# Gated delta-rule attention with a routed feed-forward: 128 blocks written out with constant waits, and the queries' rows moved by POOL's queue

## What is computed

```python
q = short_conv(x @ Wq)                      # 8 heads of 128, 4-tap causal convolution, then silu
k = short_conv(x @ Wk)                      # 3 keys for each token and head
v = short_conv(x @ Wv)                      # 3 values for each token and head
q, k = l2norm(q) * d ** -0.5, l2norm(k)
for each token t:                           # state S: 128x128 for each batch and head
    S = S * exp(g[t])
    for i in range(3):
        S = S + beta[t, i] * outer(k[t, i], v[t, i] - k[t, i] @ S)
    o[t] = q[t] @ S
o = rmsnorm(o) * rms_weight * silu(x @ Wg)
x = layernorm(x + o @ Wo)
x = layernorm(x + experts(x))               # 8 experts of width 816, the best 2 for each token
```

## Time and profile before

| what | us |
|---|---|
| median of 3 runs | 4982.57 |
| lowest and highest run | 4980.44, 4993.09 |
| span of the profiled execution | 4978.8 |
| PE, DVE, ACT, POOL busy in it | 4230.5, 3658.3, 3285.0, 1648.1 |
| first and last `gate` of the 128 blocks | 133.9, 3943.2 |

### The profile page before, as it was taken

One profiled execution on the slowest core, in us unless ns is written; L12 is line 12 of the kernel. 1 busy time (PEld: TensorE's weight loads), 2 busy tenths in 40 slices (PEclk: granted clock), 3 DMA queues, 4 the chain that ended last, 5 costly groups with the idle time before them and its releaser, 6 DMA issues. The chain is left out here.

```text
span 4978.8 us, 148669 instructions
## 1 busy us (share of the span) xinstructions
PE 4230.5 (85%) x47876; PEld 3759.0 (75%) x47876; DVE 3658.3 (73%) x10194; ACT 3285.0 (66%) x9028; POOL 1648.1 (33%) x1615
## 2 busy tenths in 40 slices
PE   2889988989898888898888898889889867599992
PEld 1788878888887777788788787888878745488882
DVE  6888888888888778788888788888888722344446
ACT  3777777777777677777777777777777611255552
POOL 3434333334433333343334343333434202200004
PEclk6999999999999999999999999999999877699996
DMA  6232223222223333222222222322222133366664
GB/s 234 69 95 73 66 77 86 79 70 77 77 71 70 76 77 70 70 77 79 82 75 77 77 67 77 92 76 67 75 77 75 43 88 108 123 236 227 230 236 140
DMA packets 363269, 490.64 MB, mean 99 GB/s; under 512 B 94080, under 2 KB 308096, under 8 KB 343680
## 3 DMA queue, kind: packets, MB, share of 16 engines
q1 hardware_dynamic: 304784, 437.06, 29.8%
q10 hardware_dynamic: 51568, 27.04, 1.9%
q0 software_dynamic: 6144, 16.79, 1.1%
HBM read 352.02 MB, written 107.75 MB: 92 GB/s over the span
## 5 line engine op out<-in xcount | busy, mean ns | idle before, releaser
L1134 DVE SCALAR_TENSOR_TENSOR conv_acc<-bank,c_cur,conv_acc 128x256 f32<-128x256 f32 x2688 | 1265.9, 477 | 274.3 <-ACT conv_acc L944 261.2
L692 PE MATMUL bank<-x_cur,w_cur 128*128 128x259 f16 (+1 forms) x6144 | 913.2, 288 | 29.4 <-DVE v_rows L1122 26.3
L1329 POOL TENSOR_TENSOR squares<-kq_t 128x768 f32<-128x768 f32 x128 | 187.7, 1467 | 1909.4 <-ACT kq_t L955 1909.4
L1195 DVE CAST_PREDICATED xs_lev<-mask,bank 128x256 f16<-128x256 uint16 x1536 | 662.2, 431 | 198.1 <-PE bank L756 174.4
L1002 ACT ACTIVATE invt<-bank 128x256 f16<-128x256 f32 x1280 | 509.7, 398 | 400.3 <-issue 374.5
L993 ACT ACTIVATE inv<-bank 128x256 f16<-128x256 f32 x1536 | 607.0, 395 | 167.8 <-PE bank L768 158.1
L692 PEld LDWEIGHTS bank<-x_cur,w_cur 128*128 128x128 f16 (+1 forms) x6144 | 577.7, 102 | 124.7 <-DVE v_rows L1122 27.2
L780 PE MATMUL bank<-invt,xs_lev 128*128 128x64 f16 x5120 | 379.9, 199 | 309.4 <-ACT invt L1002 305.2
L780 PEld LDWEIGHTS bank<-invt,xs_lev 128*128 128x128 f16 x5120 | 293.2, 101 | 341.5 <-ACT invt L1002 254.2
L944 ACT ACTIVATE conv_acc<-bank,c_cur 128x256 f32<-128x256 f32 x896 | 425.3, 475 | 156.5 <-PE bank L692 149.4
L824 PE MATMUL bank<-w_sol,k_rows 128*128 128x128 f32 x2048 | 474.6, 315 | 4.5 <-ACT w_sol L1012 4.1
(11 more groups left out here) (241 smaller groups left out, 10672.6 us busy)
## 6 DMA issues: line engine op xcount, KB each, us to landing
w_cur<-w_parts_scratch SPq DMA_DIRECT2D x128, 1024.0 KB, 7.1
ew<-e_parts_scratch SPq DMA_DIRECT2D x117, 896.0 KB, 6.2
x_cur<-x_parts_scratch SPq DMA_DIRECT2D x128, 259.0 KB, 7.0
x_slots<-no_rows SPq DMA_DIRECT2D x128, 256.0 KB, 7.1
e_parts_scratch<-e_pair SPq DMA_DIRECT2D x96, 224.0 KB, 6.0
o_rows<-w_sol ACTq DMA_DIRECT2D x512, 32.0 KB, 4.6
y_scratch<-y_buf SPq DMA_DIRECT2D x128, 128.0 KB, 6.3
y_in<-y_scratch SPq DMA_DIRECT2D x32, 512.0 KB, 4.1
```

The costliest lines, as they stand in the source:

```text
L692: last = mm(bank[i % 2][:, 0:PW], w_cur[k.i % 2][:, wp, kt, c * P:(c + 1) * P].bitcast(BF16 if wp else F16), x_cur[k.i % 2][:, xp, kt, 0:P ...
L1134: v.scalar_tensor_tensor(acc, bank[at % 2][:, i:i + TB], c_cur[k.i % 2][:, c, i:i + 1], acc, ALU.mult, ALU.add).then_inc(tap_step.sem if i ...
L1195: v.copy_predicated(half(xs_lev[g][l - 1][:], l, 0), half(mask4[:, l], l, 0).bitcast(U16), packed(halves(LEVX), l)).then_inc(x_kept.sem, 1)
```

## The change

The change does three things. Every engine's 128 blocks are written out, so all counts and addresses are constants, and the registers and loops are gone. The three copies for each block (`c_cur`, `g_cur`, `t_cur`) go, and their readers read `conv_sb`, `g_parts` and `tables` themselves; SP's additional waits and counts go with them. And `move_outputs` moves from ACT's order to POOL's, between `g_rows` and `square`, with the same transfers and the same waits.

```diff
 class Block:
-    def __init__(self, i, m, s, size):
-        self.i, self.m, self.size = i - s, m, size
-        self.n = i - s if m is None else size * m + (i - s)
-        self.runs = m is not None or 0 <= i - s < NIT
+    def __init__(self, n):
+        self.n = self.i = n
+        self.runs = 0 <= n < NIT
+        self.h, self.place = n % H, n % (B * H) * NTB + n // (B * H)
...
-            def run_bodies(eng, body):
-                assert NIT % UNROLL == 0 and UNROLL >= STAGES
-                for i in range(UNROLL):
-                    body(*blocks(i, None, UNROLL))
-                with eng.Fori(1, NIT // UNROLL) as m:
-                    for i in range(UNROLL):
-                        body(*blocks(i, m, UNROLL))
-                for i in range(NIT, NIT + STAGES - 1):
-                    body(*blocks(i, None, UNROLL))
+            def run_bodies(body):
+                for i in range(NIT + STAGES - 1):
+                    body(*blocks(i))
...
                         sp.dma_start(w_cur[res][:].rearrange("p a b c -> p (a b c)"), w_dram[h]).then_inc(loaded[res], 16)
-                        sp.dma_start(c_cur[res][:], conv_sb[:, h]).then_inc(loaded[res], 16)
-                        sp.dma_start(g_cur[res][:], g_parts[:].rearrange("p n a -> p (n a)")[:, bass.ds((head * NTB + tb) * UN, UN)])\
-                            .then_inc(loaded[res], 16)
...
-                    def body(tb, head, new=True):
-                        n = B * H * tb + head
-                        if new:
-                            done(sp, stated, 7, n - 8)
-                            sp.sem_inc(sp_waited, 1)
-                            sp.dma_start(t_cur[head % 8][:].rearrange("p a b -> p (a b)"),
...
                     def load_next(tb, head):
                         n = B * H * tb + head
                         done(sp, projected, 7, n - 1)
-                        sp.sem_inc(sp_waited, 1)
                         done(sp, tapped, 6, n - 1)
-                        sp.sem_inc(sp_waited, 1)
-                        at_least(sp, g_made, n)
-                        sp.sem_inc(sp_waited, 1)
...
-                    @at_stage
-                    def move_outputs(k):
-                        done(act, sol_kept, 7, k.n)
-                        at_least(act, scaled, k.n - 1)
-                        act.sem_inc(act_waited, 1)
-                        for c in range(4):
-                            act.dma_start(o_rows[k.i % 2][c * CH:(c + 1) * CH], w_sol[k.i % 2][96:128, c::4, :]).then_inc(moved[k.i % 2], 16)
...
                         keep_t(4, 0, k1)
-                        move_outputs(k3)
                         keep_tt(4, 0, k1)
...
+                    @at_stage
+                    def move_outputs(k):
+                        done(pool, sol_kept, 7, k.n)
+                        at_least(pool, scaled, k.n - 1)
+                        for c in range(4):
+                            nc.gpsimd.dma_start(o_rows[k.i % 2][c * CH:(c + 1) * CH], w_sol[k.i % 2][96:128, c::4, :]).then_inc(moved[k.i % 2], 16)
...
                         square_q(k1)
                         g_rows(k0)
+                        move_outputs(k3)
                         square(k0)
```

More of the change, by code:

```diff
@@ L67 @@
 STORED = 5
-UNROLL = 32
 WR = 3
@@ L461, in done @@
             def done(eng, count, key, n, *more):
-                if not isinstance(n, int) or n >= 0:
+                if n >= 0:
                     eng.wait_ge(count.sem, count.upto(max((key,) + more, key=lambda k: count.upto(k, NIT // 2)), n))
@@ L530, in build, with blocks @@
             class Block:
[L533 to L536 removed]
+                def __init__(self, n):
+                    self.n = self.i = n
+                    self.runs = 0 <= n < NIT
+                    self.h, self.place = n % H, n % (B * H) * NTB + n // (B * H)
                 def turn(self, ring):
[L540 to L543 removed]
+                    return self.n // ring
+            def blocks(i):
+                return [Block(i - s) for s in range(STAGES)]
             def at_stage(f):
@@ L649, in _ @@
                     load(0, 0, 0)
[L650 to L657, removed]
-                            load_next(tb, head)
[L659 to L667, removed]
+                    for n in range(NIT):
+                        tb, head = n // (B * H), n % (B * H)
+                        if n + 1 < NIT:
+                            load_next(tb, head)
+                        outputs(tb, head)
+                        pieces(tb, head)
+                    for i in range(STORED):
                         outputs(NTB, i, new=False)
@@ L929, in _ @@
                     pe.wait_ge(zeroed, 1)
-                    run_bodies(pe, body)
+                    run_bodies(body)
                 @block.scalar
@@ L1105, in _ @@
                     act.wait_ge(zeroed, 1)
-                    run_bodies(act, body)
+                    run_bodies(body)
                 @block.vector
@@ L1300, in body @@
                         mask_x(2, 0, k0)
-                    run_bodies(dve, body)
+                    run_bodies(body)
                 @block.gpsimd
@@ L1309, in g_rows @@
                     def g_rows(k):
-                        pool.wait_ge(loaded[k.i % 2], 64 * (k.turn(2) + 1))
                         done(pool, tt_made, "decays", k.n - 1)
-                        tt(g_upto[:], g_cur[k.i % 2][0:96, :, None].broadcast_to([96, UN, CH]),
+                        tt(g_upto[:], g_parts[0:96, k.place, :, None].broadcast_to([96, UN, CH]),
                            uptob[0:96, None, 0:CH].broadcast_to([96, UN, CH]), ALU.mult).then_inc(g_made, 1)
@@ L1381, in body @@
                         scale_outputs(k3)
-                    for head in range(B * H):
-                        body(0, head, *blocks(head, None, B * H))
-                    with pool.Fori(1, NTB) as tb:
-                        for head in range(B * H):
-                            body(tb, head, *blocks(head, tb, B * H))
-                    for i in range(NIT, NIT + STAGES - 1):
-                        body(None, i, *blocks(i, None, B * H))
+                    for i in range(NIT + STAGES - 1):
+                        body(*((i // (B * H), i % (B * H)) if i < NIT else (None, i)), *blocks(i))
         attention_scope.close()
```

52 lines of the change are left out of this document (18 added, 34 removed).

## The result

| | before | after |
|---|---|---|
| median of 4 runs, us | 4981.5 | 5201.1 |
| lowest and highest | 4950.0, 4993.1 | 5184.7, 5216.3 |
| span of the profiled execution | 4978.8 | 5214.5 |
| last `gate` of the 128 blocks | 3943.2 | 4173.3 |

The changed kernel is slower: the ratio is 1.045, with an interval of 1.041 to 1.049. I had forecast 4685 us, faster. The loss lies in the blocks. (Further down, the kernel "squares later" has its time from its three runs within 1.5% of its fastest; its profile is of the fourth, slower one, 4967 us.) `gate` now runs from 133.9 to 4173.3 us, so the blocks take 4039.4 us, 230 more than the earlier trace rows give.

What follows compares the result with a forecast made beforehand. The prediction took ACT's issuing of the moves, with PE's slow clock, and the transfers' landing as the bound. Block gain 252 plus written-out blocks 43 made 295 us off 4978.8, so 4684 span, forecast 4685 us, range 4540 to 4850.

Steps and rivals of the forecast that it cites:

- What bounds the kernel: In the blocks, the 8.1 us from first move issue to squaring: ACT's work, delayed by issuing and slow clock, and the transfers.
- ACT without the moves: Without issuing, ACT's copy starts 3.30 us earlier and ACT reaches the squaring 4.5 us after the first issue, not 8.1.
- POOL issues the moves: POOL's four issues before its squares, at most 1.26 us each, fit its 14.51 us of idle time at no cost.
- My estimate of 5430: By the skill page's 3.1 us a POOL step, rows would land at 12 us, giving some 5430 us; no separate chance.
- When the rows land: POOL steps of 1.1 us put the fourth issue at 3.3 us; with 2.8 us of landing, rows land at 6.1 us.
- the transfers land as late as ACT's: Rival, chance 0.17: landing stays 4.6 us, rows come at 7.9 us, a block gains 0.2 us, time 4915 us.
- The gain of a block: First issue to squaring shrinks from 8.1 to 6.1 us: 2.0 us a block, 252 us in 126 blocks.
- slower: Rival, chance 0.08: POOL's issues become the serial part; 2.0 us steps and 3.5 us landing give 5116 us.
- The clock: After PE's shorter stall of about 1.2 us, in place of 2.4, the clock was assumed to stay at its upper level.
- back to 4875: Failure case: the clock still falls after the shorter stall, costing up to 1.5 us a block, 190 us in all.
- Written-out blocks: Removing the loops' two jumps saves 13 us, and half of 60 us in the other loop steps 30: 43 us together.
- Fewer transfers on SP: Three of SP's nine issues a block go, of 2 to 16 KB; worth nothing, since SP is ahead of the others.

Runs made afterwards that it cites:

- squares later: Changed kernel, but ACT squares the moved rows seven instructions later, with PE's norms and DVE's sum later too: 4912.1 us, 0.982 of the kernel before.
- the kernel with held loads: Changed kernel, but SP issues the next block's input and weight loads only after a block's four moves have landed: 4445.3 us, 0.890 of the kernel before.
- the experiments with matmuls in the stall: Changed kernel with channel 4's projection, just ahead of PE's stall, computed four times or twice (18 or 6 matmuls more): 4959.8 and 5079.4 us.
- the kernel without moves: Changed kernel without the four moves, the rows' buffers set to one, so the outputs are wrong: 4520.2 us, 0.903 of the kernel before.

## Why the prediction was wrong, by its steps

*What bounds the kernel.* Right: the stretch from the first issue to the squaring, and that under ACT's stall the landing lies at nearly the same time. Incomplete: I took DVE for the next bound, 26.4 us a block. The floor is PE's: 3201 us busy in 127 blocks is 25.2, and the kernel with held loads has a median step of 25.2. It is so low because PE's busy time itself shrinks at full clock, 3400 to 3201.

*ACT without the moves.* Right: the copy came early, the old waits of 374.5 and 305.2 us are gone, and ACT arrives 4.0 us after the first issue (median), where I took 4.5. Ten instructions of ACT stand between the moves' old place and the squaring, not eleven.

*POOL issues the moves.* Mis-sized in the good direction: a step of 0.54 us, not 1.1. The indirect transfer was a poor neighbour for a direct one. The squares weren't late (9.4 us after the first issue in the block shown, 10.1 before in that of the earlier trace rows). The Trainium skill's SBUF — State Buffer page ("A bandwidth-pool intuition that's wrong") has a transfer by POOL that takes about 620 ns alone take about 3100 ns beside a VectorE copy. My estimate of 5430 took that as the step between issues. Nothing of the kind shows here: no issue of the 512 took over 0.774 us, and with the load held the landing has a median of 1.8 us, though VectorE is busy for 3123 of 3262 us.

*When the rows land.* This step failed first. I put "2.8 us" from issue to landing, with 0.4 us for the load; it was 4.7 in the median and 5.9 for the fourth. What sets it is SP's load (with what SP issues behind it), not who issues: with the load held, POOL's lands in 1.8 us and ACT's in 1.9. The rows I leaned on the earlier trace rows compared POOL's transfers with SP's in another stretch and of another size. The Trainium skill (DMA: Bandwidth & Descriptors, "Issuing engines are not separate DMA queues") says that transfers of all engines run on the same 16 DMA engines; the trace agrees, with 4.7 against 4.6 us. In the prediction this was the rival "the transfers land as late as ACT's", to which I gave 0.17.

*The gain of a block.* By my own sum the measured landing leaves 8.1 - 7.5 = 0.6 us a block, some 76 us, and that rival, with 0.2 us, said 4915. The kernel is 286 us slower than even this. So the landing alone explains no loss. The chance of "slower", 0.08, was for another mechanism, long issues by POOL, and that one didn't happen.

*The clock.* This step failed second, and it decided the sign: "I assume that so short a stall leaves the clock at its upper level". The stall wasn't short. ACT arrives 3.3 us earlier than before (4.0 in place of 7.3 us after the first issue) and the rows 0.5, so ACT's wait for them grows from 0.9 to 3.4 us a block, and PE stands 357 / 110 = 3.2 us in place of 2.4. And the dips of the clock are longer (8.4 us against 4.0 on average) and more. I had priced the case "back to 4875", with the clock no worse than before; the experiments with matmuls in the stall show that the dearer clock is worth at least the 241 us that they give back. PE's additional busy time, 187 us, is part of that.

*Written-out blocks.* 43 us predicted, 26 measured. The jumps' 13 us are in it; of the other 60 us, of which I had taken half, some 13 came back.

*Fewer transfers on SP.* At nothing, in the sum, and nothing speaks against it. The profile seems to say that `w_cur` lands 7.1 us after its issue before and 10.8 after. But before, four transfers count on one semaphore, and the profile gives the counts to them in the order of issue. The last of the four, the 2 KB of `g_cur`, lands 9.9 us after its own issue, and the last packet of `w_cur` ends 9.9 us after the issue of `w_cur` before and 10.1 after (medians). The load takes as long in both.

What stays open: why the dip after the stall at L746 is so much longer than after the one at L780. The matmuls that follow differ, among them 16 of one column each (L658), and the place of the stall in the block does; no run separates the two. And whether `w_cur` delays the instructions that PE waits for: that the stalls without a producer begin while it is in flight fits this, and the packets show what PE waited for, but not what held them up.

## What to carry to other kernels

Before moving small transfers to another queue, look at what large transfer is in flight when they go out, and when it lands: the issuer changed nothing in the landing, and the order against the load changed it from 1.8 to 7.2 us. One wait of SP, on a queue that has time, was worth 756 us against the changed kernel, 11% against the one before.

A stall of PE is priced by how it changes the clock afterwards, too. Compare PE's busy time for the same matmuls in both kernels, beside the granted clock: where both differ, as here by 187 us and 0.07, the clock is a good part of the cost, and putting filler matmuls in the stall tests that in one run.

## What was not expected of the hardware

- 18 matmuls more in a block made the kernel 241 us faster (5201 to 4960), with ACT's wait unchanged.
- The clock stood at its lower level for 10 us in which PE was busy for 10.00.
- Four transfers of 32 KB, issued with a load of 1.3 MB, landed in 7.2 us; 4.7 us behind it, in 4.7; with the load held, in 1.8 (medians).
- PE stopped for 1.2 to 5.7 us with no producer late, 30 times in the kernel without moves, and 12 times when the loads were held too; each stop ended 1.2 to 1.6 us after a 16 KB packet of instructions had ended.
